# Two mixture-of-experts layers and two cross layers on one core: the shared steps of the second token half moved behind the routed blocks

## The reference

```
probs = softmax(x @ Wr); routing_weights, selected = top_k(probs, 2)
moe_out = sum over the selected experts of weight * (silu(x @ wg) * (x @ wu)) @ wd
shared = sigmoid(x @ Wsg) * ((silu(x @ Sg) * (x @ Su)) @ Sd)
```

## Time and profile before

| | before |
|---|---|
| runs, us | 792.45, 791.6, 788.49 (median 791.6) |
| profiled execution, its own time / span, us | 790.86 / 788.7 |
| PE busy | 678.8 us, 86% |
| DVE busy | 535.4 us, 68% |
| ACT busy | 412.2 us, 52% |
| POOL busy | 377.0 us, 48% |
| mean granted PE clock, share of full | 0.931 |
| chain that ended last: PE, DVE, DMA | 15%, 4%, 1% of the span |
| POOL, context's low part (L1483), one operation | 2.87 us |

### The profile page before, as it was taken

The page is one execution under the profiler, slowest core; times in us unless marked ns, Lnnn a source line. Parts: engine busy times, 40 slices in busy tenths (PEclk is TensorE's granted clock), DMA queues, the critical chain, the costliest instruction groups (busy, mean ns, idle before and its releaser), DMA issues. The chain is left out here.

```text
span 788.7 us, 11629 instructions
## 1 busy us (share of the span) xinstructions
PE 678.8 (86%) x3578; PEld 519.5 (66%) x3578; DVE 535.4 (68%) x1142; ACT 412.2 (52%) x923; POOL 377.0 (48%) x332
## 2 busy tenths in 40 slices
PE   7698878969969953799999999999979869999970
PEld 2244333558847743689999888988967747777750
DVE  5999999734823226789899888888886863422226
ACT  2897764233214422677777567766754225444430
POOL 0699878142447730634354332233222147777750
PEclk9799989989969985999999999999998979999995
DMA  4647411240453312111204203000005412333327
GB/s 143 283 148 254 186 67 40 77 161 1 160 173 103 106 53 101 49 52 61 75 27 144 78 21 118 1 1 2 20 2 188 193 47 91 105 100 104 105 82 266
DMA packets 33117, 78.61 MB, mean 100 GB/s; under 512 B 5529, under 2 KB 14370, under 8 KB 32034
## 3 DMA queue, kind: packets, MB, share of 16 engines
q1 hardware_dynamic: 26176, 59.37, 21.1%
q0 software_dynamic: 6720, 18.36, 7.7%
q10 hardware_dynamic: 162, 0.14, 0.1%
HBM read 59.17 MB, written 18.68 MB: 99 GB/s over the span
## 5 line engine op out<-in xcount | busy, mean ns | idle before, releaser
L1729 DVE COPY g_hT<-psum 88x256 f32<-88x256 f32 x70 | 29.5, 421 | 114.4 <-PE psum L1315 114.4
L1305 PE MATMUL psum<-ex,g_xT 128*128 x280 | 99.6, 480 | 0.9 <-ACT g_xT L1410 0.5
L2029 ACT ACTIVATE a_p_exp<-psum,a_nmax 128x256 f32<-128x256 f32 x128 | 59.6, 471 | 56.5 <-DVE a_nmax L2197 56.5
L1489 POOL DMA_INDIRECT g_rows<-rows,f_token_of x70 | 68.1, 973 | 34.1 <-issue 17.1
L1495 POOL DMA_INDIRECT planes<-xn,f_target_of x70 | 69.5, 993 | 30.8 <-ACT xn L1459 15.6
L2128 POOL TENSOR_TENSOR a_rr<-a_ss,eps 128x8 f32<-128x8 f32 x32 | 6.6, 206 | 156.8 <-DVE a_ss L2178 156.8
L611 POOL TENSOR_TENSOR m_dbu<-m_du,m_b_all 128x1024 f32<-128x1024 f32 x31 | 73.7, 2393 | 9.5 <-DVE m_du L697 6.9
L705 DVE TENSOR_TENSOR_SCAN m_hst<-psum,m_dbu 128x1024 f32<-128x1024 f32 x32 | 73.0, 2281 | 0.0
L1324 PE MATMUL psum<-ex,g_hT 88*128 x280 | 71.8, 379 | 0.0
L1305 PEld LDWEIGHTS psum<-ex,g_xT 128*128 128x128 f32 x280 | 54.7, 198 | 21.3 <-issue 3.9
L357 PE MATMUL psum<-m_hc,ident 128*128 128x512 f32 x128 | 64.4, 627 | 0.0
(11 more groups left out here) (282 smaller groups left out, 1885.7 us busy)
## 6 DMA issues: line engine op xcount, KB each, us to landing
ex<-in_ex SPq DMA_DIRECT2D x24, 608.0 KB, 6.2
m_b_all<-b_rows SPq DMA_DIRECT2D x8, 1024.0 KB, 5.6
held<-planes SPq DMA_DIRECT2D x6, 1024.0 KB, 7.4
k_raw<-m_side SPq DMA_DIRECT2D x16, 256.0 KB, 2.0
a_keys<-k_raw SPq DMA_DIRECT2D x16, 256.0 KB, 2.6
w_raw<-in_moe SPq DMA_DIRECT2D x9, 384.0 KB, 3.9
fold_in<-in_w_fold SPq DMA_DIRECT2D x8, 384.0 KB, 3.3
a_raw<-in_w_pair SPq DMA_DIRECT2D x8, 384.0 KB, 3.3
```

Source lines behind the costliest of these rows:

```text
L1305: mm = pe.matmul(act_bank(b), xT[:, b % 2, k * P:(k + 1) * P], ew[:, bass.ds(at + k * 2 * FE, 2 * FE)], start=(k == 0), stop=(k == KD - 1))
L1489: pool.indirect_dma_start(rows[:, b % XG, :], None, mix.rows, bass.IndirectOffsetOnAxis(ap=token_of[:, b:b + 1], axis=0)).then_inc(mix.row ...
L2029: ins = act.activation(pe_[:, n % 2, m, :], bank(hh)[:, tile * L:(tile + 1) * L], ACT.Exp, bias=nmax[:, n % 2, m:m + 1], accum_out=rsum[:, ...
```

## The change

In both mixtures `closing`, the second half's shared steps, stands behind the routed blocks on PE, ACT, POOL and DVE; `opening` keeps the first half's. The hidden buffers are two deep in mixture 0 too (three before). The shared gate is no longer multiplied into the hidden values: its logit is a ninth column of the routing logits, ACT makes one tanh of eight columns, and `residual` scales the down sums by it, tile by tile. The residual of the first half comes ahead of the blocks, that of the second behind the last down; `combine` asks only for the residual of the first half where it runs before. Logits are made for each half in both mixtures. The high and low parts of the second half's x are made among the first blocks. The second combine of mixture 0 moves from attention into the closing steps. The exponents of mixture 0 move among the blocks. SP loads chunks 4 and 5 ahead of the second half's rows, experts 0 to 6 in one go, and clears the mixer's semaphores behind the opening steps. The experts' and other buffers lie at other places in SBUF.

The core of the diff (PE, then ACT, POOL, DVE, SP):

```diff
+                pe.wait_ge(mix.wr_in, 16)
+                half_logits(0)
+                pe.wait_ge(s.lo, KD)
+                if gated:
+                    rest.tensor(pe)
+                    gate_up(J0)
+                    gate_up(J0 + 1)
+                    turned()
+                else:
+                    gate_up(J0)
+                    rest.tensor(pe)
+                    turned()
+                    gate_up(J0 + 1)
+                half_logits(1)
+                for j in opening:
+                    if j + 2 < JB:
+                        gate_up(j + 2)
+                    if j - J0 == RANK_AT and gated:
+                        ranked()
+                    if j - J0 == MAPPED_AT and gated:
+                        mapped()
+                    if j == J0:
+                        pe.wait_ge(mix.logits_read, len(EACH))
+                    down(j)
                 if not gated:
+                    ranked()
+                    mapped()
...
-                pe.wait_ge(mix.x_back, 4)
+                pe.wait_ge(mix.x_back, 2)
+                pe.wait_ge(mix.rank_read, 1)
...
+                pe.wait_ge(s.lo, 2 * KD)
+                gate_up(JB)
+                gate_up(JB + 1)
+                pe.wait_ge(mix.y_s, B0 + NB)
+                for j in closing:
+                    if j + 2 < J1:
+                        gate_up(j + 2)
+                    if after is not None and j == J1 - 2:
+                        for k in range(KD):
+                            norm_turned(pe, sh, after, 0, k, NEXT[k])
+                    down(j)
```

with `RANK_AT, MAPPED_AT = ((0, 4), (2, 2))[m]`. ACT and POOL:

```diff
+                for j in opening:
                     if not gated and j == J0 + 1:
+                        kept_full()
+                    gated_by(j)
+                    if gated and j == J0 + 1:
+                        kept_full()
                     for c in beside[j]:
                         w.gate_up_high(act, c)
                     for c in beside[j - 1]:
                         w.down_high(act, c)
+                    hidden_high(j)
+                    if gated and j == J0 + 3:
+                        shared_gate()
...
+                    if i in (2, 3):
+                        high_half(i - 2)
+                    if i == 6:
                         exponents()
...
+                for j in closing:
+                    gated_by(j)
+                    if after is not None and j == J1 - 1:
+                        for k in range(KD):
+                            norm_hi(act, sh, after, 0, k, NEXT[k])
+                    hidden_high(j)
...
+                if gated:
+                    pool.wait_ge(sh.c_hi_s, 1)
+                    pool.tensor_tensor(sh.c_lo[:, :], sh.ctxT[:, :], sh.c_hi[:, :], ALU.subtract)
                 norm_deviation(pool, sh, s, 1)
+                for j in opening:
...
+                    if gated and j == JB - 1:
+                        pool.wait_ge(mix.rows_out, 32)
+                        pool.wait_ge(mix.idx_ready, 1)
+                        gathered(0)
+                    hidden_low(j)
...
+                for j in closing:
+                    if after is not None and j == J1 - 2:
+                        norm_deviation(pool, sh, after, 0)
+                    hidden_low(j)
```

DVE and SP:

```diff
+                    if h == 0:
+                        dve.wait_ge(mix.gate_ready, 1)
+                        dve.tensor_scalar(gate[:, :], gate[:, :], 0.5, 0.5, ALU.mult, ALU.add).then_inc(mix.gate_ready, 1)
+                    dve.wait_ge(mix.gate_ready, 2)
+                    for t in range(h * TPH, (h + 1) * TPH):
+                        ins = dve.scalar_tensor_tensor(x[:, t, :], bank(t // 2)[:, (t % 2) * DM:(t % 2 + 1) * DM], gate[:, t:t + 1],
+                                                       x[:, t, :], ALU.mult, ALU.add)
...
+                rest.vector(dve)
+                norm_statistics(dve, sh, s, 1)
+                route_groups(0)
+                scaled()
+                hidden(J0)
+                route_pick(0)
+                hidden(J0 + 1)
+                route_groups(1)
+                route_pick(1)
+                hidden(J0 + 2)
+                slots_found()
+                if gated:
+                    hidden(J0 + 3)
+                pairs_placed(0, PAIRS)
+                if gated:
+                    hidden(J0 + 4)
+                tokens_found()
+                if gated:
+                    hidden(J0 + 5)
                 block_experts()
+                residual(0)
+                targets_found()
+                shifted()
...
+                    if i in (4, 5):
+                        low_half(i - 4)
...
+                hidden(JB)
+                hidden(JB + 1)
                 if after is not None:
+                    hidden(JB + 2)
+                    mix.combine(dve, sh, 0, 2)
+                    hidden(JB + 3)
                     norm_statistics(dve, sh, after, 0)
                     norm_scaled(dve, sh, after, 0)
+                    hidden(JB + 4)
+                    mix.combine(dve, sh, 1, 2)
+                    hidden(JB + 5)
                     for k in range(KD):
                         norm_lo(dve, sh, after, 0, k, NEXT[k])
+                    residual(1)
+                else:
+                    mix.combine(dve, sh, 0, 2)
+                    hidden(JB + 2)
+                    mix.combine(dve, sh, 1, 2)
+                    residual(1)
+                    mix.combine(dve, sh, 2, 4)
+                    mix.combine(dve, sh, 3, 4)
...
-                    rows_kept(1)
                     for c in range(C0 + 4, C1):
                         w.load(sp, c)
+                    rows_kept(1)
                     for i in range(2):
                         sp.wait_ge(pre.keys_in[i], SIDE_OUT)
-                    for e in range(3):
+                    for e in range(experts - 1):
                         mix.expert_in(sp, e)
                     sp.wait_ge(w.dn_lo_s, C1)
...
+                    mix.expert_in(sp, experts - 1)
                     pre.load(sp)
+                    sp.wait_ge(w.down_s, JB)
+                    for signal in rest.held:
+                        sp.sem_clear(signal)
```

More of the change, by code:

```diff
@@ L849 @@
 EX0, FRONT0 = 37344, 29944
-EX0_AT = (33696, 34912, 36128, 7680, 8896, 2176, 3392, 960)
+EX0_AT = tuple(28832 + 1216 * n for n in range(7)) + (9216,)
 START = (0, len(ORDER0))
@@ L1051, in moe_block @@
     J0, J1 = START[m], STOP[m]
-    steps = range(J0, J1)
+    JB = J0 + (J1 - J0) // 2
+    opening, closing = range(J0, JB), range(JB, J1)
     split_ahead = (3, 2)[m]
[L1054 to L1061, removed]
+    beside = {j: [c for c in range(C0 + split_ahead, C1) if prepared(c) == j] for j in range(J0 - 1, JB)}
+    RANK_AT, MAPPED_AT = ((0, 4), (2, 2))[m]
     PAIRS = NT * K
@@ L1225, in gate_up @@
                                     mm.then_inc(done, 1)
-                                beside_them((what * KD + k) * 3 + i)
                 def down(j):
                     c, h = STEPS[j]
-                    first = j == min(i for i in steps if STEPS[i][1] == h)
+                    fresh = j in (J0, JB)
                     pe.wait_ge(mix.h_lo_s, n(j))
@@ L1237, in down @@
                                       (h_hi[:, j % HS, tok], h_lo[:, j % HS, tok]),
[L1238 removed]
+                                      (w.dn_hi[c], w.dn_lo[c]), fresh and t % 2 == 0, False)
                     mm.then_inc(w.down_s, 1)
[L1241 to L1247, removed]
[L1249 to L1256 removed]
                 def half_logits(h):
@@ new lines, in residual @@
+                def residual(h):
+                    dve.wait_ge(w.down_s, (JB, J1)[h])
+                    if not gated:
+                        for q in range(2 * h, 2 * h + 2):
+                            xs = x[:, 2 * q:2 * q + 2, :].rearrange("p t f -> p (t f)")
+                            dve.tensor_tensor(xs, xs, bank(q), ALU.add).then_inc(mix.x_back, 1)
+                        return
+                    if h == 0:
[5 more added lines that the diff above has]
+                                                       x[:, t, :], ALU.mult, ALU.add)
+                        if t % 2:
+                            ins.then_inc(mix.x_back, 1)
@@ L2167, in _ @@
             def _(dve):
-                moe[0].combine(dve, sh, 1)
+                dve.wait_ge(moe[0].x_back, 4)
                 norm_statistics(dve, sh, s, 1)
```

245 lines of the change are left out of this document (61 added, 184 removed).

## The result

The changed kernel takes 756.04 us (median of 754.39, 755.79, 756.3, 756.55) against 792.03 for the kernel before on the same chip: 0.9548 of it, 95% interval 0.9512 to 0.9584. The forecast was 758.0, in a range of 747 to 775. The profiled execution took 754.39 us with a span of 752.6, against 790.86 and 788.7: 36.1 us less span, where the sum had 32.9.

A forecast was written before the change was run, and what follows sets the result against it. PE was taken to bound each mixture's dense stage, with PE waiting in the tails. The terms -37.5 + 0.9 + 6.9 - 2.0 - 4.0 + 0.3 + 2.5 gave -32.9 from 790.86, so 758.0 us, range 747 to 775.

The forecast's parts named there:

- Front of mixture 0: Stage start to first routed matmul: six shared steps (25.1 us) and other work leave, 80.3 us before; -37.5, bounds -40 and -28.
- POOL's detour: Mixture 0's front: the last low part waits behind gather 0 on POOL, adding 1.3 us before the first routed matmul.
- Blocks of mixture 0: Routed blocks: exponents moved among them cost 0.6 us, high and low parts 0.3; +0.9, bounds 0 and 3.
- Tail of mixture 0: Behind the blocks to attention: six closing steps lengthen 23.1 us to 30.0; +6.9, bounds +5 and +12.
- Attention's start: The second combine (3.3 us) no longer stands there, so the first sum of squares comes sooner; -2.0, bounds -2.7 and 0.
- Front of mixture 1: DVE sets it; two hidden and the block experts leave the stretch between places and gather; -4.0, bounds -5 and 0.
- its blocks: Mixture 1's routed blocks: four small operations for high and low parts are added; +0.3, bounds 0 and 1.2.
- Tail of mixture 1: Behind the blocks: hidden 2 ahead of the second combine, 0.7, residual waiting for the last down, 0.5; +2.5, bounds +1, +6.
- Rival 1: Closing steps don't hide DVE work: nine POOL low parts each stop DVE 1.29 us, 769 to 770 us; chance 0.15.
- Rival 2: The routing chain sets mixture 0's front, which ends at 200 to 205; 768 to 773 us; chance 0.14.
- Rival 3: Slower by PE's clock: each shared step at low level costs 4.19 us more, all eighteen give 833; chance 0.05.

The follow-up runs named there:

- rows_first: The changed kernel with the second half's rows stored ahead of the loads of chunks 4 and 5 again; 756.45 us, 0.9572 of before.
- copies_behind: The changed kernel with rows stored ahead of the chunk loads and ACT's copies of the second half's transposes behind chunk 4's split; 763.31 us, 0.9647 of before.
- changed_again: The changed kernel, unaltered, run once more on another group's chip; 755.66 us, 0.9571 of before.
- tail1: The changed kernel with the third hidden ahead of the first combine in DVE's queue in mixture 1's closing; 757.8 us, 0.9594 of before.
- low_on_dve: The changed kernel with the nine low parts of both closings made by DVE instead of POOL; 760.08 us, 0.9613 of before.
- the filled run: The changed kernel with tail1's order and unused products of zeros on PE in mixture 0's front and behind its closing's last down; 752.33 us, 0.9524 of before.

## Why the prediction was right, point by point

**Front of mixture 0, -37.5: right, by two errors that cancel.** Measured -36.9. The sum counts from 147.0, and the stage began at 146.29 here; from its start the xn end at 9.8 us (9.5 predicted), the second logits at 14.5 (13.7), and the map's copy stands at 33.7 (31.6), since PE's first products behind the logits are partly at the lower level (granted 0.75). The 2.1 us came back behind the map: from the gather to the first routed matmul it took 7.45 us, not 8.1, and POOL's detour of 1.3 us doesn't lie on the path, because the gather is issued ahead of the low part and the residual ends at 188.0, as late as the rows arrive. So the hit to a tenth of a microsecond (42.9 against 42.8) is luck.

The reason "chunk 4 is loaded ahead of the second half's rows now, so its wait goes" holds for ACT: the load is issued at 148.58, and the split at 158.68 waits for nothing, where in rows_first it waits 1.56 us. It leaves out a second change that does it for PE: rows_first undoes the order and nothing happens, copies_behind undoes both and brings 4 to 6 us. So the copies' place on ACT, ahead of the split, is enough by itself to take the wait off PE's path. Whether the load order would have been enough by itself, as the prediction has it, was not run.

**Blocks of mixture 0, +0.9: wrong sign, 1.5 us off.** The exponents cost what was forecast: the two blocks around them take 3.07 and 2.58 us instead of 2.49 each, 0.67 together. ACT's timeline in the kernel after:

```profile
207.00 1.28 ACT L1397 ACT_TABLE_LOAD   x1
208.29 0.26 ACT L1397 ACTIVATE f_ex<-f_ex 128x64 f32<-128x64 f32 x1
208.56 1.28 ACT L1426 ACT_TABLE_LOAD   x1
209.86 0.32 ACT L1426 ACTIVATE g_act<-psum 128x176 f32<-128x176 f32 x1
```

The two table loads with Exp between them fill 2.86 us of ACT, and a block's slack swallows most of it. By the rule of the Trainium skill, "ScalarE: Activation LUTs", What ACT_TABLE_LOAD costs (1283 ns for a load and 1380 ns for a drain), the trace agrees on the load and shows no drain: Exp starts as the load ends. What I hadn't seen is the start: the second block distance fell from 3.08 to 1.84 us. Before, PE had waited 4.54 and 1.45 us for the first rows, now 1.69 us, and the granted clock in the first 6 us of the blocks is 0.51 before and 0.72 after:

```profile
227.29:233.29 6.00, 6.00 (x14) 3.74 (x15) 0.38 (x2) 1.02 (x3) 1.63 (x2) 0.51 0.50 168
...
189.19:195.19 6.00, 6.00 (x19) 3.85 (x20) 1.17 (x4) 1.51 (x5) 3.63 (x4) 0.72 0.26 66
```

No run changed these waits alone.

**Tail of mixture 0, +6.9: right**, +6.7, and 29.9 us in every run that has this code. PE is busy 89% of it, a little under the 90% that I named, and the last down starts 25.7 us behind the blocks (26.1 predicted). The clears carry 3.3 us of it (2.5 in the sum). Two mishaps hide in the right total: one combine is 1.0 us longer beside a low part, and a low part 2.3 us longer beside a combine. PE, which sets this tail, stood only 0.71 and 0.21 us for them, at 272.46 and 274.37.

**Attention's start, -2.0:** the first sum of squares begins 2.5 us after DVE's start instead of 5.2, so -2.7, the bound; of these, 1.25 us are left at the last transposes of the softmax, 277 us later, against the 2.0 forecast. The stage shows -3.7, but the other 2.5 us are luck. They lie between these transposes and mixture 1's first matmul, where the granted clock was 0.70 before and 1.00 after:

```profile
588.88:598.89 10.01, 8.78 (x42) 7.68 (x43) 5.81 (x18) 3.33 (x7) 1.01 (x1) 0.70 0.00 0
...
555.63:563.15 7.52, 6.29 (x43) 5.36 (x43) 5.76 (x18) 3.34 (x7) 1.01 (x1) 1.00 0.00 0
```

The same code takes 7.52 us for this stretch in changed_again and 10.0 in rows_first and tail1, so the change doesn't set it.

**Front of mixture 1, -4.0, and its blocks, +0.3:** -4.9 and +0.1; other runs of the same code in mixture 1 give -2.5 to -5.1 for the front, so the hit is within what executions differ by. The first gather comes 35.0 us behind the stage's start instead of 40.2.

**Tail of mixture 1, +2.5: mis-sized; it measured +4.5.** The failed step is "DVE's queue gets hidden 2 (0.7) ahead of the second combine, and the residual must wait for the last down, about 0.5". I priced the third hidden by its own length, not by what waits behind it: PE stood 3.92 us, and the last combine ends 25.8 us behind the blocks instead of 24. Moving it ahead of the first combine gives back about 1.5 us (28.1 to 29.0, to 27.2), and the collision with the low part is 1.0 of the rest.

**The rivals.** Rival 1 is real as a mechanism and wrong as a price: of nine low parts three met a combine, not each, and the loss of 1.0 us fell twice on DVE and 2.3 us once on POOL, not 1.29 nine times. The Trainium skill, "SBUF — State Buffer", SBUF: two separate sides, has a VectorE operation with two SBUF inputs and a GpSimd operation lock each other out of a shared port: whichever starts first keeps it for its whole instruction. That these two engines are the pair, low_on_dve bears out. Two of the overlaps fit one instruction at a time as well, POOL losing 0.3 us (a combine operation is 0.41) and DVE 1.0 (a low part is 1.29). The third doesn't: POOL lost 2.3 us there, the time of more than five operations of that combine. Rival 2 did not come: the front is 42.9. Rival 3 did not come in the closing (granted 1.00 over 30 us), but a small form of it stood in the front, where the low level costs 1.6 to 4.3 us, by the filled run.

## What to carry to other kernels

Work that depends on nothing nearby belongs where the critical engine waits, and its worth is what that wait can hold: six steps of 25.1 us filled a tail of 23 and paid 15 to 19 us, three steps in the other tail paid nothing that shows, since DVE was the chain there. When a load comes late, look at what is queued behind the waiting instruction, and not only at the load; and price an operation inserted into a queue by who waits for the one behind it. Before a move is called neutral or worth a few microseconds, compare it by stage, and the granted clock of each stage with it: executions of the same code differed by 3 us here, and 2.5 us of one stage's gain were the clock's.

## What the runs showed of the hardware that was not expected

Two things. An operation of POOL and a combine of DVE at the same time shared the loss in two ways in one kernel: DVE lost 1.04 us and POOL 0.3 (257.90 and 259.12), or POOL lost 2.3 and DVE nothing (268.85). And one and the same front took 42.3, 42.7, 42.9, 44.8, 45.0 and 45.0 us in six executions, by the clock that PE was granted: where it ran at full level from the start it was at half behind two gaps, in which PE stood for 0.9 and 1.6 us; the executions that began below full level came later to the first gap's place, had only the second gap, and were the faster ones. Products of zeros in these gaps left it at full level in the one profile taken; whether they always do was not tried.
